# A decoder layer on one core: the DMAs of the 1/std row and of the first x^T issued by ScalarE, with new instruction lists

## The reference

```
def layernorm(x): return (x - mean(x)) / sqrt(var(x) + 1e-5)

# A: one head of 128; layernorm in front of it
q, k, v = (layernorm(x) @ w for w in (w_q, w_k, w_v))
x = x + (softmax(q @ k.T / sqrt(128)) @ v * head_mask) @ w_o

# B: both sides through the same projection
xp = relu(layernorm(x) @ W.T + b);  yp = relu(ctx @ W.T + b)
x = x + softmax(where(mask, -inf, xp @ yp.T)) @ ctx

# C: gated FFN, weights ternary, activations in 127 steps
def weight_quant(w): s = 1 / mean(|w|); return clip(round(w * s), -1, 1) / s
def act_quant(x):    s = 127 / max(|x|, per token); return round(x * s) / s
def bitlinear(x, w): return act_quant(x) @ weight_quant(w).T
h = layernorm(x)
x = x + bitlinear(silu(bitlinear(h, w_gate)) * bitlinear(h, w_up), w_down)
```

## Time and profile before

| | us |
|---|---|
| median of three runs | 403.87 |
| the profiled execution | 403.0 |
| its span, from first to last instruction | 401.2 |
| TensorE busy | 367.7 (92%) |
| VectorE busy | 331.2 (83%) |
| ScalarE busy | 311.4 (78%) |
| GpSimd busy | 287.3 (72%) |

### The profile page before, as it was taken

The page is one execution under the profiler, slowest core; times in us unless marked ns, Lnnn a source line. Parts: engine busy times, 40 slices in busy tenths (PEclk is TensorE's granted clock), DMA queues, the critical chain, the costliest instruction groups (busy, mean ns, idle before and its releaser), DMA issues.

```text
span 401.2 us, 7242 instructions
## 1 busy us (share of the span) xinstructions
PE 367.7 (92%) x2098; PEld 283.6 (71%) x2098; DVE 331.2 (83%) x936; ACT 311.4 (78%) x571; POOL 287.3 (72%) x412
## 2 busy tenths in 40 slices
PE   6537789999999999999999999999999999999764
PEld 5425567897788768787878688867787787667432
DVE  4559975786899868997999798969997899999981
ACT  3138599589878996899778997788689979977861
POOL 2036897049967996899588997899478978984541
PEclk9868999999999999999999999999999999999996
DMA  8855311003321345142531435225252101431574
GB/s 284 341 193 178 98 53 55 26 7 117 87 41 29 90 97 180 36 92 63 204 72 20 98 94 186 43 55 113 87 80 65 28 14 24 123 66 28 123 142 105
DMA packets 53687, 38.50 MB, mean 96 GB/s; under 512 B 45072, under 2 KB 46736, under 8 KB 53264
## 3 DMA queue, kind: packets, MB, share of 16 engines
q1 hardware_dynamic: 53648, 38.04, 36.0%
HBM read 23.33 MB, written 4.21 MB: 69 GB/s over the span
## 4 chain that ended last, share of the span: by engine, by line
PE 55%; POOL 14%; DVE 9%; issue 7%; DMA 7%; ACT 6%; SPq 2%; POOLq 0%; ACTq 0%; DVEq 0%
PE b_bank L879 7%; PE b_bank L881 7%; PE b_bank L880 7%; PE a_bank L879 4%; PE a_bank L881 4%; PE a_bank L880 4%; PE g_bank L1033 4%; PE u_bank L1033 3%; DMA r_rows<-a_rstd 3%; PE d_bank L1042 3%; POOL c_work L601 3%; PE b_bank L992 3%; PE a_bank L926 2%; POOL c_work L642 2%; DMA c_half<-c_half 2%
## 5 line engine op out<-in xcount | busy, mean ns | idle before, releaser
L601 POOL TENSOR_TENSOR c_work<-c_work 128x512 f32<-128x512 f32 x48 | 61.8, 1293 | 13.4 <-DVE c_work L1259 10.5
L642 POOL TENSOR_SCALAR c_work<-c_work,h_q 128x1024 f32<-128x1024 f32 x32 | 36.1, 1127 | 18.1 <-DVE h_q L1278 18.1
L812 ACT ACTIVATE c_half<-c_work 128x1024 bf16<-128x1024 f32 x32 | 34.0, 1063 | 12.5 <-POOL c_work L642 12.4
L1271 DVE TENSOR_REDUCE h_max<-c_work 128x1 f32<-128x1024 f32 x32 | 38.7, 1210 | 5.7 <-POOL c_work L601 5.5
L1042 PE MATMUL d_bank<-downT,c_half 128*128 128x256 bf16 x256 | 35.0, 282 | 7.3 <-DMA c_half<-c_half 7.2
L802 ACT ACTIVATE c_work<-g_bank,c_tanh_scale 128x512 f32<-128x512 f32 x52 | 36.4, 700 | 5.0 <-PE g_bank L1033 4.6
L879 PE MATMUL b_bank<-ctx_hi,b_pT_hi 128*128 128x256 f32 x128 | 39.0, 305 | 0.1
L1259 DVE SCALAR_TENSOR_TENSOR c_work<-c_work,g_bank 128x512 f32<-128x512 f32 x52 | 35.1, 676 | 3.8 <-ACT c_work L802 3.6
L1042 PEld LDWEIGHTS d_bank<-downT,c_half 128*128 128x128 bf16 x256 | 24.7, 100 | 17.5 <-DMA c_half<-c_half 9.9
L880 PE MATMUL b_bank<-ctx_lo,b_pT_hi 128*128 128x256 f32 x128 | 36.1, 282 | 0.0
L881 PE MATMUL b_bank<-ctx_hi,b_pT_lo 128*128 128x256 f32 x128 | 36.1, 282 | 0.0
(11 more groups left out here) (245 smaller groups left out, 1275.8 us busy)
## 6 DMA issues: line engine op xcount, KB each, us to landing
ctxT_raw<-in_ctx_t SPq DMA_DIRECT2D x8, 512.0 KB, 3.5
ctx_raw<-in_ctx SPq DMA_DIRECT2D x8, 512.0 KB, 3.5
x_all<-in_x SPq DMA_DIRECT2D x7, 512.0 KB, 4.5
a_xT_raw<-in_x_t SPq DMA_DIRECT2D x7, 512.0 KB, 3.8
out<-x_all SPq DMA_DIRECT2D x7, 512.0 KB, 3.2
r_bc<-r_rows SPq DMA_DIRECT2D x8, 256.0 KB, 4.1
c_work<-in_w_gate SPq DMA_DIRECT2D x1, 1024.0 KB, 7.7
c_half<-in_w_down SPq DMA_DIRECT2D x1, 1024.0 KB, 11.0
```

What stands on the lines that cost most here:

```text
L601: pool.tensor_tensor(h[:, t % 2, half * HALF:(half + 1) * HALF], th[:, j % 2, :], up[:, j % 2, :], ALU.mult).then_inc(hs, 1)
L642: pool.tensor_scalar(h[:, t % 2, :], h[:, t % 2, :], h_q[:, t:t + 1], ROUND, ALU.mult, ALU.add).then_inc(h_rounds, 1)
L812: act.activation(h_q8[:, t % 2, :], h[:, t % 2, :], ACT.Copy, bias=-ROUND).then_inc(hqs, 1)
L1271: dve.tensor_reduce(h_max[:, one], h[:, t % 2, :], AX.X, ALU.max, apply_absolute_value=True).then_inc(h_maxes, 1)
```

## The change

The two functions `store_r` and `load_r` move from SyncE to ScalarE, with the same waits, and are issued there as steps A.rw and A.rb of ACT_ORDER. The two DMAs of x^T of tile 0 are issued by ScalarE before anything else. ScalarE so issues on a queue of its own. All five lists are written anew. PE_ORDER, DVE_ORDER and POOL_ORDER hold the same steps as before in another order; ACT_ORDER gains the 16 steps rw and rb, and SP_ORDER loses these 16 and the two of x^T.

```diff
@@ ACT_ORDER
-    A.xT0/0 A.xT1/0 W.qkv/0 A.Q/0 A.K/0 A.xT0/1 A.xT1/1 W.hi/0 A.VT/0 E.ctxT/0 A.exp0/0 A.exp1/0 B.mask/0 A.P0/0
+    A.xT0/0 A.xT1/0 W.qkv/0 A.rw/0 A.rb/0 A.Q/0 A.K/0 E.ctxT/0 W.hi/0 A.VT/0 B.mask/0 A.exp0/0 A.exp1/0 E.YP0/0
...
@@ SP_ORDER
-    W.x0/0 W.qkv/0 W.x1/0 W.bias/0 W.t0/0 W.W/0 W.t1/0 W.o/0 S.x/1 W.gate/0 S.ctxT/0 S.ctx/0 W.down/0 S.mask/0
-    W.hm/0 W.up/0 S.rw/0 S.x/2 S.xT/1 S.rb/0 S.xT/2 S.mask/1 S.ctxT/1 S.mask/2 S.x/3 S.ctx/1 S.rw/1 S.rb/1
+    W.qkv/0 W.x0/0 W.x1/0 S.x/1 W.gate/0 W.up/0 S.ctxT/0 W.W/0 W.bias/0 W.o/0 W.hm/0 W.down/0 S.mask/0 S.ctx/0
...
@@ SyncE
-            def store_r(n):
-                sp.wait_ge(a_rstds, 4 * n + 4)
...
-            def load_r(n):
-                sp.wait_ge(r_stored, 16 * n + 16)
...
-                elif name[0] == "t":
-                    c = int(name[1])
-                    sp.dma_start(a_xT_raw[:, c, :], x_t[:, 0, c, :]).then_inc(xT0_loaded[c], 16)
@@ ScalarE
+            def store_r(n):
+                act.wait_ge(a_rstds, 4 * n + 4)
+                if n > 0:
+                    act.wait_ge(r_stored, 16 * n)
+                act.dma_start(r_rows[n, :].rearrange("(p t) -> p t", t=T), a_rstd[:, n % 2, :]).then_inc(r_stored, 16)
+
+            def load_r(n):
+                act.wait_ge(r_stored, 16 * n + 16)
+                if n > 0:
+                    act.wait_ge(r_loaded, 16 * n)
+                    act.wait_ge(a_maxed, T * n)
+                act.dma_start(r_bc[:, :], r_rows[n, :].partition_broadcast(P)).then_inc(r_loaded, 16)
...
+            for c in range(DC):
+                act.dma_start(a_xT_raw[:, c, :], x_t[:, 0, c, :]).then_inc(xT0_loaded[c], 16)
             act.wait_ge(consts_set, 7)
             act.activation(table_load[:, :], neg_round[:, :], ACT.Exp)
```

More of the change, by code:

```diff
@@ L51 @@
[L51 to L55, removed]
@@ new lines @@
+    A.H/0 W.total/0 E.YP0/1 A.Y0/0 A.Y1/0 E.YP1/1 A.Q/1 A.K/1 A.V/1 A.VT/1 B.XT0/0 B.XT1/0 A.S0/1 E.YP0/2
+    B.XP0/0 B.XP1/0 A.S1/1 A.P0/1 A.S2/1 A.P1/1 B.S0/0 B.S1/0 A.S3/1 B.P0/0 B.S2/0 A.P2/1 A.P3/1 B.P1/0 B.O0/0
+    A.H/1 B.S3/0 B.P2/0 A.Y0/1 A.Y1/1 B.O1/0 B.P3/0 A.Q/2 A.K/2 B.O2/0 B.O3/0 A.V/2 B.XT0/1 B.XT1/1 E.YP1/2
+    A.VT/2 A.S0/2 B.XP0/1 B.XP1/1 A.S1/2 A.P0/2 E.YP0/3 C.u0/0 C.g0/0 A.S2/2 A.P1/2 B.S0/1 C.g1/0 A.S3/2 B.S1/1
+    C.u1/0 A.P2/2 B.P0/1 B.S2/1 A.P3/2 C.u2/0 C.g2/0 B.P1/1 B.O0/1 A.H/2 B.S3/1 C.u3/0 B.P2/1 A.Y0/2 A.Y1/2
@@ new lines @@
+SP_ORDER = """
+    W.qkv/0 W.x0/0 W.x1/0 S.x/1 W.gate/0 W.up/0 S.ctxT/0 W.W/0 W.bias/0 W.o/0 W.hm/0 W.down/0 S.mask/0 S.ctx/0
+    S.x/2 S.xT/1 S.ctxT/1 S.mask/1 S.x/3 S.mask/2 S.xT/2 S.ctxT/2 S.ctx/1 S.ctxT/3 S.xT/3 S.mask/3 S.ctx/2
+    S.xqT0/0 S.ctxT/4 S.xT/4 S.xqT1/0 S.hT0/0 S.mask/4 S.xT/5 S.ctx/3 S.hT1/0 S.xqT0/1 S.ctxT/5 S.hT2/0 S.hT3/0
+    S.xqT1/1 S.store/0 S.x/4 S.hT0/1 S.mask/5 S.hT1/1 S.ctx/4 S.xqT0/2 S.hT2/1 S.xT/6 S.hT3/1 S.ctxT/6 S.xqT1/2
+    S.store/1 S.mask/6 S.x/5 S.hT0/2 S.hT1/2 S.xqT0/3 S.ctx/5 S.hT2/2 S.hT3/2 S.xT/7 S.xqT1/3 S.ctxT/7 S.mask/7
+    S.hT0/3 S.store/2 S.x/6 S.xqT0/4 S.hT1/3 S.hT2/3 S.hT3/3 S.ctx/6 S.xqT1/4 S.store/3 S.x/7 S.hT0/4 S.hT1/4
+    S.xqT0/5 S.ctx/7 S.hT2/4 S.xqT1/5 S.hT3/4 S.hT0/5 S.hT1/5 S.xqT0/6 S.store/4 S.hT2/5 S.hT3/5 S.xqT1/6
+    S.hT0/6 S.xqT0/7 S.hT1/6 S.xqT1/7 S.store/5 S.hT2/6 S.xqT2/7 S.hT3/6 S.xqT3/7 S.hT0/7 S.store/6 S.hT1/7
+    S.hT2/7 S.hT3/7 S.store/7""".split()
@@ L420, in load_xT @@
                 sp.dma_start(a_xT_raw[:, :, :], x_t[:, n]).then_inc(xT_loaded, 16)
-            def store_r(n):
-                sp.wait_ge(a_rstds, 4 * n + 4)
-                if n > 0:
-                    sp.wait_ge(r_stored, 16 * n)
-                sp.dma_start(r_rows[n, :].rearrange("(p t) -> p t", t=T), a_rstd[:, n % 2, :]).then_inc(r_stored, 16)
-            def load_r(n):
-                sp.wait_ge(r_stored, 16 * n + 16)
-                if n > 0:
-                    sp.wait_ge(r_loaded, 16 * n)
-                    sp.wait_ge(a_maxed, T * n)
-                sp.dma_start(r_bc[:, :], r_rows[n, :].partition_broadcast(P)).then_inc(r_loaded, 16)
             def load_ctxT(n):
@@ L822, in step @@
             def step(stream, name, n):
-                if name == "hi":
+                if name == "rw":
+                    store_r(n)
+                elif name == "rb":
+                    load_r(n)
+                elif name == "hi":
                     act.wait_ge(W_loaded, 16)
```

261 lines of the change are left out of this document (125 added, 136 removed).

## The result

In one series on the same chip the changed kernel took 401.71 us (median of 7 runs, 400.44 to 402.33), the kernel before 406.10 us (7 runs, 403.52 to 407.97). The ratio is 0.9894, with an interval of 0.9859 to 0.9928: faster, by 1.1%. The forecast was 396.3 us. The profiled executions stand closer to each other, 403.0 before and 400.9 after, with spans of 401.2 and 398.9 us.

The account below looks back on a forecast made before the run. TensorE bounds the body; the start is bound by vT waiting for tile 0's row store behind SyncE's loads. 8.1 + 0.5 - 1 = 7.6 us gained gives 396.3 us, range 391.5 to 403.

Parts of the forecast that it names:

- each microsecond beyond it costs one: Tile 0's row store: landing in up to 4 us changes almost nothing; each further microsecond costs one.
- Part 1: Tile 0's row store and load on ScalarE's queue: store lands in 3.5 us, vT starts at 17.9, gaining 8.1 us.
- part 4: VectorE from vT to A.H: last W.sum moved behind A.P3, k_lo behind vT; net gain 0.5 us.
- part 5: W.scales behind hT_lo, ahead of A.Y0: from A.H to A.Q of tile 1 half a microsecond at best; taken as 0.
- parts 6 and 7: ScalarE's cost of issuing 18 DMAs, charged 1 us (0 to 3); lists in another order, taken as 0.
- part 2: Start loads, x^T and x of tile 0, attention weights first: A.Q perhaps 1 us forward; taken as nothing.
- Part 3: w_up issued earlier on SyncE: lands at about 16 us, its sum ends at about 17.3, thinly before vT.
- With a landing of over 5 us q_hi is late by the rest: ScalarE waits for tile 0's store before q_hi: free in idle time, but a landing over 5 us delays q_hi.
- A: Rival: both queues share one line, store lands at about 22.5, row at 26 as before; 404 us, chance 0.08.
- B: Rival: start gain lost again to TensorE gaps in the body or late w_up; 400.1 to 403.9 us, chance 0.09.
- C: Rival: ScalarE's waits at rw and rb stop its copies of TensorE's banks; slower, 411 us, chance 0.10.

Follow-up runs that it names:

- experiment 1: Changed kernel with SyncE issuing nothing behind w_up until the store of tile 0's row has landed; 395.91 us, ratio 0.9771.
- experiment 7: Changed kernel with SyncE holding the context and all behind it until the load of tile 0's row has landed; 399.13 us, ratio 0.9892.
- experiment 5: Changed kernel with w_gate, w_up and w_down each loaded by four DMAs with rows of 2 KB; 401.12 us, ratio 0.9909.
- experiment 4: Changed kernel with bias, w_o, head mask and mask ahead of the context and w_down on SyncE; 403.18 us, ratio 0.9933.
- experiment 2: Kernel before, its lists kept, with only tile 0's x^T and row store and load on ScalarE's queue; 403.11 us, ratio 0.9954.
- experiment 3: Changed kernel's lists with all DMAs back on SyncE, rw and rb placed by the author; 413.86 us, ratio 1.0220.

## Why the prediction was wrong

**What held.** The bound was read rightly: the row's way through DRAM set vT, and vT set the start. The rest of the run passes the start's gain on unchanged. The forecast's own condition, "each microsecond beyond it costs one", held from the landing to vT. "Faster by more than 1%", with its chance of 0.73, came true by a hair (1.1%, 0.7 to 1.4) and not by the size that it rested on.

**What was not in it.** Behind vT a microsecond is not passed on one for one, as the sum took it: beside the changed kernel, vT 4.0 us sooner gave 1.5 us at the end of A.H in experiment 1, and 6.4 us gave 1.9 in experiment 7, where late transfers have a part in it. So no run shows that a vT at 17.9 would have brought the 8.1 us.

**Part 1, the step that failed.** "I take 3.5, nearer to the median of 2.4 than to the maximum." It took 7.6 us. The median of 2.4 came from stores issued in a body where the DMA engines are busy for 30% of the time; this one is issued where they are full (1.01 and 1.04 in the windows above). Neither nearest row was near, and I weighed by distance in duration instead of by load. The terms, against the assumed ones: issue at 10.69 instead of 9.82, 0.9; landing 7.6 instead of 3.5, 4.1; load 5.2 instead of 4.1, 1.1; less 0.4 us of slack before the end of A.V that the forecast had: 5.7 us. That is about the whole miss, 400.9 against 395.4 in the profiled execution, since the other terms nearly cancel (0.1 for part 4 and 0.7 for part 5 lost, 1.2 for parts 6 and 7 won). Experiment 1 takes the landing back to 2.6 us and has 395.9 us; experiment 7 takes the load back to 3.5 and has vT at 17.1.

Of the two rules weighed there, neither gave this. By "Issuing engines are not separate DMA queues" in the Trainium skill's "DMA: Bandwidth & Descriptors" the row gains nothing but issue time; it gained 6 us of landing. By "Queues, rings and completion order" of the same page it waits for about one packet of the other queue, and a packet there is a run of descriptors, typically 9 to 17 and at most 64, not one packet of the profile's count. It waited 3.5 us and 1.40 MB for its first. That is 21 of the profile's packets on each of the 16 DMA engines, 42 in experiment 5, 45 in experiment 4 and 4 in experiment 1, so no fixed run fits; and the turns that followed went one for one (80 and 78 in experiment 2).

The late issue has a cause that part 2 held. a_rstd needs both halves of x of tile 0, and the second one landed later. VectorE's first operation on it, before, after, in experiment 2 and in experiment 3:

```profile
5.65 0.75 DVE L1086 BATCH_NORM_STATS2 a_bn<-x_all 128x6 f32<-128x256 f32 x2 [1.08 <-DMA x_all<-in_x]
...
6.95 0.76 DVE L1085 BATCH_NORM_STATS2 a_bn<-x_all 128x6 f32<-128x256 f32 x2 [0.18 <-DMA x_all<-in_x]
...
7.56 0.76 DVE L1101 BATCH_NORM_STATS2 a_bn<-x_all 128x6 f32<-128x256 f32 x2 [1.64 <-DMA x_all<-in_x]
...
5.49 0.75 DVE L1084 BATCH_NORM_STATS2 a_bn<-x_all 128x6 f32<-128x256 f32 x2 [0.24 <-DMA x_all<-in_x]
```

The place of the attention weights is not the reason: the second half stands behind the same bytes of SyncE's in both lists. With x^T on ScalarE's queue it is late with the order of before too (experiment 2), and with x^T back on SyncE's queue it is early with the new order (experiment 3). So what delays it is that x^T moves beside it on the second queue, which the prediction did not price. GpSimd finished a_rstd at 10.66, and two of its four operations for it ran for 0.61 and 1.02 us instead of 0.2 and 0.7, beside VectorE's a_xT_lo. I had put the issue at the end of wqkv_hi, and forgot that the operand could be later.

**Part 2**, taken as nothing: TensorE's wait for wqkv_lo went from 4.0 to 3.6 us. Right but for the late issue just told. **Part 3**: w_up landed at 13.2, not at 16, and its sum ended at 21.1, since VectorE stood 4.6 us for q_hi; vT waited for the row another 2.5 us, so it hid. "With a landing of over 5 us q_hi is late by the rest" happened, and cost nothing as long as the row was later still. **Part 4**, 0.5 us: from vT to the end of A.H 17.47 us before, 17.07 after, 0.4. The scores ran again at 1.2 GHz (granted 0.56 from 24.4 to 30.0 us), after another 6.7 idle us. In experiment 1, with 2.4 us of waiting for vT, they ran at 2.4 GHz from 24 to 30 us, but from 34 to 39 the granted clock was 0.50 and A.H's products came every 0.43 us instead of 0.23; vT to the end of A.H took 19.6 us. **Part 5**, zero: from A.H to A.Q of tile 1 6.57 us before, 7.26 after, 0.7 lost. The sum of the steps was right, but W.scales has no fixed price: 1.8 to 5.1 us by what GpSimd does meanwhile. **Parts 6 and 7**, 1 us and zero: the rest went from 351.2 to 351.0. The sixteen steps on ScalarE cost nothing that shows; ScalarE's only waits for the store of any tile are the 8.3 us before q_hi and 0.8 before a k_hi.

The ledger: 2.4 + 0.4 - 0.7 + 0.2 = 2.3 us of span, forecast 8.1 + 0.5 + 0 - 1 = 7.6.

**The rivals.** A expected a landing at 22.5 and vT at 26; a landing of 7.6 us lies halfway between it and the forecast. The two lines are separate, but not free of each other, and I had no case between them. The range reached up to 403 and did hold the time. B's condition, 4 us of new gaps in the body, is not met. C did not occur.

**What stays open.** What sets the 3.5 us before the first packet. It is the same with 339 and 680 packets ahead, 1.9 with the context issued together with the store, 4.3 with the small transfers first, and 1.1 to 1.8 when SyncE has nothing behind w_up. And what sets the load of the row beside other loads. It took 3.5 us with nothing of SyncE's passing, 4.1 with 0.6 MB, 5.3 to 5.9 with 0.9 to 1.0, 5.2 with 1.5 and 6.3 to 6.9 with 2.1 to 2.2. More passes beside a longer load as well, so these numbers alone do not show which is the cause.
